# Layer 1's softplus begun inside layer 0's scan, its polynomial on POOL, B's rows before the slot fill, and filler products on PE

## The chip, the cores and the metric

The kernel runs on one core of a Trainium2 chip. The metric is device time in microseconds, median of several runs. Engines are named as in the profile: PE (TensorE, matrix products), DVE (VectorE), ACT (ScalarE), POOL (GpSimd), SP (issues most DMAs).

## What is computed

Four layers, each a residual attention-like part and a residual feed-forward part, each gated by a tanh. Tokens: 4 sequences of 256, so 1024 tokens, 256 features; everything is fp32. Layers 0 and 1 begin with a Mamba scan over `ctx_1024`:

```python
x = silu(conv(in_proj(ctx)) + conv_b)                 # u, 256 channels
dt_low, B, C = split(x_proj(x))                       # 8, 16 and 16 rows
delta = softplus(dt_proj(dt_low) + dt_b)
A = -exp(A_log)                                       # 256 x 16
state = state * exp(delta * A) + (delta * u) * B      # over 256 steps, for each of 16 states
y = (state * C).sum(states) + D * u
x_out = x + tanh(g) * y * silu(layernorm(x_in))
```

Behind them come a mixture of 16 experts (4 chosen, a router with sigmoid), a ternary feed-forward, an attention with 32 heads and an fp8 feed-forward, a second attention, and a mixture with 2 of 16 experts and a softmax router, of which only the chosen token rows are computed.

## The kernel before

The code is written engine by engine: each engine has one list of instructions, and they meet at counting semaphores alone (`wait_ge`, `then_inc`). Nothing reorders; what stands first on an engine runs first. Channels lie on the 128 partitions in two halves (`t` = 0, 1), tokens along the free dimension, so a half is 128x1024.

Both scans have 16 states. For each state and half ACT writes the decays exp(delta A) to PSUM (`decays`, L557), POOL multiplies delta u by the state's row of B (L588), which a DMA has spread over all partitions, DVE scans (L604) and weighs with C (L613), and PE adds up (L510). Layer 1's scan does not depend on x: it runs inside layer 0's mixture of experts (`mixture_*`), with POOL's L668 and L675 and DVE's L642 and L652.

Between them stands a chain. DVE forms y (L683, L687, two halves), PE turns it (L528, `mamba_tail_tensor`), DVE adds it to x and takes statistics (L691, L295, L299), POOL the inverse deviation (L312, L313), DVE normalises (L305, `ln_apply`), PE turns that (L322), ACT copies it to ZT (L330), PE makes the router's products (L1101) and the shared expert's (L733), and DVE chooses the experts (from L1142).

Softplus has three parts. ACT takes e = exp(-|d|) and e/3 - 1/2 (L436 to L441) and later ln(1 + e) (L445). DVE makes a mask e < 2^-7 and a polynomial (L453, L455, L456), puts the polynomial into the logarithm where the mask is set (L460), adds max(d, 0) (L461) and multiplies by u (L462); L466 is D u. For layer 1 ACT begins when the states of layer 0 are turned, and DVE's part stands between `ln_apply` and the router. POOL's first L668 waits for `du_done` and for a row of B. SP issues the rows of B and C for layer 1 behind `slot_dram <- slots`, a fill of 4 MB of DRAM that is used in the last mixture.

In the last mixture the router comes first again (L322 turns, the same L1101, softmax on DVE), the shared expert (L1279, L1289) runs on PE meanwhile, POOL scatters rows by indirect DMA (L1267), and 31 tiles of 128 slots go through turn (L1373), up (L1382), turn (L1391, L1392) and down products.

An fp32 product on PE is two instructions in the trace, a transpose one.

## Time and profile before

| what | value |
|---|---|
| median of 3 runs | 962.38 us (962.22 to 966.5) |
| profiled execution, its own time | 962.05 us |
| its span | 959.8 us |
| busy: PE, DVE, ACT, POOL | 85%, 70%, 46%, 45% of the span |
| chain that ended last: PE, DVE, issue, POOL, DMA, ACT | 50%, 29%, 9%, 5%, 3%, 3% |

The span is from the first to the last instruction of the profiled execution. The chain that ended last is followed back from the last instruction, at each step to what released it; its shares say where the time is set, while a busy share only says that an engine had work.

### The profile page before, as it was taken

The page shows a single profiled execution, that of the slowest core. Times are in us where ns is not written, and L with a number is a line of the kernel's source. Part 1 is how long each engine was busy: PE and PEld are TensorE (multiplying, and loading weights), DVE is VectorE, ACT ScalarE, POOL GpSimd, SP SyncE. Part 2 cuts the span into 40 slices and gives each one's busy share as a digit, 9 for nine tenths or more (in the row PEclk, how much of TensorE's full clock was granted, in tenths as well). Part 3 has the DMA queues.
Part 4 walks back from the last instruction along what each step waited for, and adds up shares of the span by engine and source line. Part 5 has one row for each costly group of instructions (what it writes and reads, how often), then busy time and mean ns, then how long its engine had stood idle before and what let it go on. Part 6 is the DMA issues. An engine that isn't in the chain of part 4 may idle for free.

```text
span 959.8 us, 12466 instructions
## 1 busy us (share of the span) xinstructions
PE 814.8 (85%) x4178; PEld 525.4 (55%) x4178; DVE 667.2 (70%) x1012; ACT 440.8 (46%) x826; POOL 433.2 (45%) x297
## 2 busy tenths in 40 slices
PE   7978989937999999982898979998937988979992
PEld 3323333335888877772776445554525865546661
DVE  5888999799999999997465467778537275312222
ACT  5752322350777767662555626665505422113331
POOL 3025666312599988883397012435301431513331
PEclk9977788867999999995899879999969986979997
DMA  6121122754122222211001113341161010151114
GB/s 224 50 86 68 66 66 76 295 203 131 44 88 89 88 88 87 88 44 43 35 1 34 52 39 93 98 134 36 56 238 33 1 67 1 71 194 49 46 44 158
DMA packets 28532, 81.71 MB, mean 85 GB/s; under 512 B 3360, under 2 KB 17200, under 8 KB 27088
## 3 DMA queue, kind: packets, MB, share of 16 engines
q1 hardware_dynamic: 26080, 73.25, 22.4%
q0 software_dynamic: 2256, 6.18, 1.8%
q10 hardware_dynamic: 144, 1.57, 0.4%
q8 instruction: 34, 0.56, 0.2%
q14 instruction: 18, 0.15, 0.1%
HBM read 65.64 MB, written 17.35 MB: 86 GB/s over the span
## 4 chain that ended last, share of the span: by engine, by line
PE 50%; DVE 29%; issue 9%; POOL 5%; DMA 3%; ACT 3%; DVEq 1%; SPq 0%; POOLq 0%; ACTq 0%
DVE M L652 6%; DVE M L642 6%; PE ps L510 6%; PE ps L1382 5%; PE ps L1752 4%; PE ps L1756 4%; PE ps L501 3%; PE ps L1794 3%; PE ps L384 3%; PE ps L934 3%; DVE F L873 2%; POOL ZT L1017 2%; PE ps L1401 2%; POOL slot_scratch L1267 2%; DVE stats L295 1%
## 5 line engine op out<-in xcount | busy, mean ns | idle before, releaser
L788 PE MATMUL ps<-W,ZT 128*128 128x256 f32 x512 | 122.1, 382 | 0.0
L588 POOL TENSOR_TENSOR M<-M 128x1024 f32<-128x1024 f32 x32 | 75.3, 2355 | 88.3 <-DVE M L462 47.4
L668 POOL TENSOR_TENSOR M<-N,M 128x1024 f32<-128x1024 f32 x32 | 81.9, 2561 | 55.4 <-DMA M<-dbl_scratch 39.1
L1823 ACT ACTIVATE N<-ps 128x512 f32<-128x512 f32 x128 | 69.5, 594 | 75.7 <-PE ps L1756 75.7
L788 PEld LDWEIGHTS ps<-W,ZT 128*128 128x128 f32 x512 | 93.5, 192 | 10.4
L675 POOL TENSOR_TENSOR W<-W,M 128x1024 f32<-128x1024 f32 x32 | 86.3, 2695 | 5.9 <-DVE M L652 5.9
L1844 DVE TENSOR_REDUCE W<-ps 128x4 f32<-128x1024 f32 x64 | 78.1, 1221 | 8.9 <-PE ps L1756 5.9
L1752 PE MATMUL ps<-M,W 32*128 32x256 f32 x512 | 74.0, 418 | 10.8 <-DVE W L1850 5.7
L510 PE MATMUL ps<-M,ident 128*128 128x512 f32 x128 | 75.7, 745 | 6.9 <-DVE M L613 6.9
L604 DVE TENSOR_TENSOR_SCAN M<-ps,M 128x1024 f32<-128x1024 f32 x32 | 73.3, 2291 | 9.0 <-ACT ps L557 8.4
L1756 PE MATMUL ps<-W,M 32*128 32x256 f32 x512 | 79.1, 402 | 0.0
L642 DVE TENSOR_TENSOR_SCAN M<-ps,M 128x512 f32<-128x512 f32 x64 | 77.8, 1216 | 0.8 <-issue 0.6
L557 ACT ACTIVATE ps<-M 128x1020 f32<-128x1020 f32 x32 | 35.7, 1115 | 81.6 <-DVE M L604 81.6
L810 PE MATMUL ps<-W,F 128*128 128x256 f32 x256 | 65.9, 380 | 1.0 <-ACT F L851 1.0
L652 DVE TENSOR_TENSOR M<-M 128x512 f32<-128x512 f32 x64 | 66.4, 1037 | 0.0
L1752 PEld LDWEIGHTS ps<-M,W 32*128 32x128 f32 x512 | 44.4, 191 | 38.2 <-DVE W L1850 19.2
L1007 POOL TENSOR_TENSOR M_rounded<-Z,M_rounded 128x512 fp32r<-128x512 f32 x28 | 40.4, 1446 | 51.4 <-ACT M_rounded L984 51.4
L934 PE MATMUL ps<-N_rounded,W_rounded 128*128 128x512 f32 x224 | 59.6, 413 | 3.2 <-DVE N_rounded L918 3.2
L1475 POOL DMA_INDIRECT ytok_scratch<-Z,M x31 | 29.8, 962 | 71.6 <-ACT Z L1437 71.6
L510 PEld LDWEIGHTS ps<-M,ident 128*128 128x128 f32 x128 | 29.0, 239 | 55.3 <-issue 43.6
L846 ACT ACTIVATE F<-F 128x128 f32<-128x128 f32 x128 | 55.5, 482 | 0.3
L1454 DVE COPY M<-ps 128x128 f32<-128x128 f32 x31 | 9.1, 292 | 66.4 <-PE ps L1392 66.4
(288 smaller groups left out, 1708.8 us busy)
## 6 DMA issues: line engine op xcount, KB each, us to landing
...
slot_scratch<-in_slots SPq DMA_DIRECT2D x1, 3999.0 KB, 18.6
...
```

The source lines that it names most:

```text
L510: last = nc.tensor.matmul(ps[:, 2 * t + half, :], ident[:], hC[:, t, half * HALF:(half + 1) * HALF], start=(n == 0), stop=True, skip_group ...
L588: nc.gpsimd.tensor_tensor(dBu[:, t, :], du[0][:, t, :], Bb[:, par, :], ALU.mult).then_inc(S("dBu_rdy"), 1)
L604: nc.vector.tensor_tensor_scan(hst[:, t, :], dAp, dBu[:, t, :], 0.0, ALU.mult, ALU.add).then_inc(S("h_rdy"), 1)
L642: nc.vector.tensor_tensor_scan(hst[:, t, at], dAp1[:, at], dBu[:, t, at], 0.0, ALU.mult, ALU.add).then_inc(S("h1_rdy"), 1)
L652: nc.vector.tensor_tensor(hC[:, t, at], hst[:, t, at], Cb[:, par, at], ALU.mult).then_inc(S("hC1_rdy"), 1)
L668: nc.gpsimd.tensor_tensor(dBu[:, t, :], du[1][:, t, :], Bb[:, par, :], ALU.mult).then_inc(S("dBu1_rdy"), 1)
L675: nc.gpsimd.tensor_tensor(u[1][:, t, :], u[1][:, t, :], hC[:, t, :], ALU.add).then_inc(S("y1_acc"), 1)
L788: last = nc.tensor.matmul(ps[:, UBANK[j % 2], e * DIM:(e + 1) * DIM], ZT[:, c, t * P:(t + 1) * P], gu[:, c, 2 * j + e, :], start=(c == 0), ...
L934: last = nc.tensor.matmul(ps[:, 4 + 2 * kind + q % 2, :], gu[:, c, u, kind * P:(kind + 1) * P], part[:, c, half * HALF:(half + 1) * HALF], ...
L1752: return nc.tensor.matmul(ps[:, b, q * SEQ:(q + 1) * SEQ], qst[32 * b:32 * b + 32, h, q * P:(q + 1) * P], kst[32 * b:32 * b + 32, h, :], s ...
L1756: return nc.tensor.matmul(ps[:, 4 + n % 3, k * SEQ:(k + 1) * SEQ], kst[32 * b:32 * b + 32, e, k * P:(k + 1) * P], qmax[32 * b:32 * b + 32, ...
L1844: nc.vector.tensor_reduce(spots[:, 2 * which:2 * which + 2], ps[:, 2 * which:2 * which + 2, :].rearrange("p b (q k) -> p b q k", q=2), AX. ...
```

## The change

On ACT the loop over layer 0's states is unrolled, and after states 10, 11 and 12 it takes one step of layer 1's softplus for both halves. The mask and the polynomial of layer 1 are on POOL, behind its last product of the first scan. The logarithm stands on ACT behind the two Silu of the tail; the first half's L460 and L461 stand on DVE before the tail and its L462 before the turned states, the rest where the softplus was. The rows of B for layer 1 are loaded once POOL is done with the rows of layer 0, with a semaphore of their own; the slot fill and `moe` are issued near the start, behind the first two rows of B; the rows of C wait for `du_done`. `stay_busy` puts products whose result nobody reads into eight waits of PE. On POOL three waits use the chain's semaphore.

```diff
+        log1 = two(W[:, w_free:w_free + 2 * TOK])
...
+        def stay_busy(bank, n):
+            for _ in range(n):
+                nc.tensor.matmul(ps[:, bank, :], ident[:], ctxT[:, 0:HALF], start=True, stop=True)
...
@@ mamba0_sync
+            sp.dma_start(moe[:, 0:MOE_COLS - 32], a["moe"]).then_inc(S("ld_w3"), 16)
+            sp.dma_start(slot_dram, a["slots"]).then_inc(S("ld_w3"), 16)
             with sp.Fori(1, NSTATE // 2) as i:
...
+        def mamba1_first_rows(sp):
             sp.wait_ge(S("dbl_out"), 32)
             sp.wait_ge(S("dBu_rdy"), 2 * NSTATE)
             for par in range(2):
-                load_rows(sp, 1, par, par)
+                sp.dma_start(Bb[:, par, :], row1(par)).then_inc(S("b1_in"), 16)
...
+        def softplus1_exponent(act, step):
+            for t in range(2):
+                if step == 0:
+                    nc.scalar.activation(Cb[:, t, :], delta[1][:, t, :], ACT.Abs).then_inc(S("sp_exp"), 1)
+                elif step == 1:
+                    act.wait_ge(S("sp_exp"), 6 + t + 1)
+                    nc.scalar.activation(log1[:, t, :], Cb[:, t, :], ACT.Exp, scale=-1.0).then_inc(S("sp_exp"), 1)
                 else:
+                    act.wait_ge(S("sp_exp"), 8 + t + 1)
+                    nc.scalar.activation(du[1][:, t, :], log1[:, t, :], ACT.Identity, scale=1.0 / 3.0,
+                                         bias=col("mhalf")[:, 0:1]).then_inc(S("sp_exp"), 1)
+        def softplus1_logarithm(act):
+            for t in range(2):
+                act.wait_ge(S("sp_poly"), t + 1)
+                nc.scalar.activation(log1[:, t, :], log1[:, t, :], ACT.Ln, bias=1.0).then_inc(S("sp_ln"), 1)
+        def softplus1_gpsimd(pool, link):
+            for t in range(2):
+                e, q = log1[:, t, :], du[1][:, t, :]
+                pool.wait_ge(S("sp_exp"), 10 + t + 1)
+                link(nc.gpsimd.tensor_scalar(Cb[:, t, :], e, 2.0 ** -7, None, ALU.is_lt))
+                link(nc.gpsimd.tensor_tensor(q, q, e, ALU.mult))
+                link(nc.gpsimd.tensor_scalar(q, q, 1.0, None, ALU.add))
+                nc.gpsimd.tensor_tensor(q, q, e, ALU.mult).then_inc(S("sp_poly"), 1)
+        def softplus1_delta(dve, link, t):
+            d, log = delta[1][:, t, :], log1[:, t, :]
+            dve.wait_ge(S("sp_ln"), 2 + t + 1)
+            link(nc.vector.copy_predicated(log, Cb[:, t, :].bitcast(mybir.dt.uint32), du[1][:, t, :]))
+            link(nc.vector.scalar_tensor_tensor(d, d, 0.0, log, ALU.max, ALU.add))
...
-            with act.Fori(1, NSTATE) as n:
-                decays(n, False)
+            for n in range(NSTATE):
+                decays(n, n == 0)
+                if 10 <= n < 13:
+                    softplus1_exponent(act, n - 10)
...
@@ sync
             sp.dma_start(dn, a["dn0"]).then_inc(S("ld_w0"), 16)
+            mamba1_first_rows(sp)
             sp.wait_ge(S("xm_done"), BATCH)
             sp.dma_start(tern, tern_dram).then_inc(S("tern_in"), 16)
-            sp.dma_start(moe[:, 0:MOE_COLS - 32], a["moe"]).then_inc(S("ld_w3"), 16)
-            sp.dma_start(slot_dram, a["slots"]).then_inc(S("ld_w3"), 16)
+            sp.wait_ge(S("du_done"), 4)
             mamba1_sync(sp)
@@ tensor
             mamba0_tensor(pe)
+            stay_busy(6, 5)
             mamba_tail_tensor(pe, 0)
+            stay_busy(3, 4)
             ln_tensor(pe, 1, 0)
+            stay_busy(3, 2)
             pe.wait_ge(S("ld_w0"), 80)
...
             pe.wait_ge(S("x_done"), NT)
+            stay_busy(2, 13)
             mamba_tail_tensor(pe, 1)
+            stay_busy(3, 4)
             pe.wait_ge(S("xm_done"), 2 * BATCH)
             ternary_tensor(pe)
+            stay_busy(7, 2)
...
             attn3_tensor(pe)
+            stay_busy(1, 3)
             ln_tensor(pe, 7, 5)
...
             pe.wait_ge(S("x_done"), 4 * NT)
             pe.wait_ge(S("expert_of"), 1)
+            stay_busy(0, 5)
             turn_rows(0)
```

Lines of the changed kernel are numbered anew. DVE behind the last weighing of the first scan (L613), before:

```order
L613 TENSOR_TENSOR M<-M,ps 128x1024 [waits y_acc,cb_rdy,h_rdy]
L683 SCALAR_TENSOR_TENSOR M<-M,cols,ps 128x1024 [waits y_acc,tanh_done]
L687 TENSOR_TENSOR M<-M 128x1024 [waits sz_done,dve_chain]
L683 SCALAR_TENSOR_TENSOR M<-M,cols,ps 128x1024
L687 TENSOR_TENSOR M<-M 128x1024 [waits sz_done,dve_chain]
L691 SCALAR_TENSOR_TENSOR X<-ps,tanh_g,X 128x512 [waits y_tr] x2
```

and in the changed kernel, where L667, L742, L746 and L752 are the old L613, L683, L687 and L691:

```order
L667 TENSOR_TENSOR M<-M,ps 128x1024 [waits y_acc,cb_rdy,h_rdy]
L515 COPY_PREDICATED W<-M,N 128x1024 [waits sp_ln]
L516 SCALAR_TENSOR_TENSOR N<-N,W 128x1024 [waits dve_chain]
L742 SCALAR_TENSOR_TENSOR M<-M,cols,ps 128x1024 [waits y_acc,tanh_done,dve_chain]
L746 TENSOR_TENSOR M<-M 128x1024 [waits sz_done,dve_chain]
L742 SCALAR_TENSOR_TENSOR M<-M,cols,ps 128x1024
L746 TENSOR_TENSOR M<-M 128x1024 [waits sz_done,dve_chain]
L519 TENSOR_TENSOR N<-N,W 128x1024
L752 SCALAR_TENSOR_TENSOR X<-ps,tanh_g,X 128x512 [waits y_tr,dve_chain]
```

L515 and L516, the old L460 and L461 of half 0, stand before the tail, and L519, the old L462, before the turned states.

DVE behind `ln_apply`, before, ten operations up to the second half's product:

```order
L453 TENSOR_SCALAR M<-M 128x1024 [waits sp_exp]
L455 TENSOR_TENSOR M<-M 128x1024 [waits sp_exp,dve_chain]
L456 SCALAR_TENSOR_TENSOR M<-M 128x1024 [waits dve_chain]
L453 TENSOR_SCALAR M<-M 128x1024 [waits sp_exp,dve_chain]
L455 TENSOR_TENSOR M<-M 128x1024 [waits sp_exp,dve_chain]
L456 SCALAR_TENSOR_TENSOR M<-M 128x1024 [waits dve_chain]
L460 COPY_PREDICATED M<-M 128x1024 [waits sp_ln,dve_chain]
L461 SCALAR_TENSOR_TENSOR N<-N,M 128x1024 [waits dve_chain]
L462 TENSOR_TENSOR N<-N,W 128x1024 [waits dve_chain]
L466 TENSOR_SCALAR W<-W,cols 128x1024 [waits dve_chain]
L460 COPY_PREDICATED M<-M 128x1024 [waits sp_ln]
```

and in the changed kernel (L522 is the old L466):

```order
L522 TENSOR_SCALAR W<-W,cols 128x1024
L515 COPY_PREDICATED W<-M,N 128x1024 [waits sp_ln]
L516 SCALAR_TENSOR_TENSOR N<-N,W 128x1024 [waits dve_chain]
L519 TENSOR_TENSOR N<-N,W 128x1024 [waits dve_chain]
L522 TENSOR_SCALAR W<-W,cols 128x1024 [waits dve_chain]
```

The polynomials and half 0 are gone from there.

POOL behind its last product of the first scan (L588), before:

```order
L312 TENSOR_SCALAR vpe<-mv 128x4 [waits ln_mv]
L313 TENSOR_TENSOR rstd<-vpe,cols 128x4 [waits pool_chain]
L312 TENSOR_SCALAR vpe<-mv 128x4 [waits ln_mv]
L313 TENSOR_TENSOR rstd<-vpe,cols 128x4 [waits pool_chain]
L668 TENSOR_TENSOR M<-N,M 128x1024 [waits bc0,du_done]
L668 TENSOR_TENSOR M<-N,M 128x1024
```

and in the changed kernel, where L313, L314 and L727 are the old L312, L313 and L668:

```order
L507 TENSOR_SCALAR M<-W 128x1024 [waits sp_exp]
L508 TENSOR_TENSOR N<-N,W 128x1024 [waits pool_chain]
L509 TENSOR_SCALAR N<-N 128x1024 [waits pool_chain]
L510 TENSOR_TENSOR N<-N,W 128x1024 [waits pool_chain]
L507 TENSOR_SCALAR M<-W 128x1024 [waits sp_exp]
L508 TENSOR_TENSOR N<-N,W 128x1024 [waits pool_chain]
L509 TENSOR_SCALAR N<-N 128x1024 [waits pool_chain]
L510 TENSOR_TENSOR N<-N,W 128x1024 [waits pool_chain]
L313 TENSOR_SCALAR vpe<-mv 128x4 [waits ln_mv]
L314 TENSOR_TENSOR rstd<-vpe,cols 128x4 [waits pool_chain]
L313 TENSOR_SCALAR vpe<-mv 128x4 [waits ln_mv]
L314 TENSOR_TENSOR rstd<-vpe,cols 128x4 [waits pool_chain]
L727 TENSOR_TENSOR M<-N,M 128x1024 [waits du_done,b1_in] x2
```

Eight operations of 128x1024 stand ahead of the inverse deviation, and the first L727 waits for half 0's `du_done` instead of half 1's.

## Rows read from the trace of the kernel before

**Rows 1.** Timeline of DVE: start, us, engine, line, idle before, releaser.

```profile
192.25 1.28 DVE L683 SCALAR_TENSOR_TENSOR M<-M,cols,ps 128x1024 f32<-128x1024 f32 x1 [2.20 <-PE ps L510]
...
198.45 1.60 DVE L691 SCALAR_TENSOR_TENSOR X<-ps,tanh_g,X 128x512 f32<-128x512 f32 x2 [1.21 <-PE ps L528]
...
207.90 0.69 DVE L453 TENSOR_SCALAR M<-M 128x1024 f32<-128x1024 f32 x1
...
214.39 1.36 DVE L460 COPY_PREDICATED M<-M 128x1024 f32<-128x1024 uint32 x1
...
217.04 1.23 DVE L462 TENSOR_TENSOR N<-N,W 128x1024 f32<-128x1024 f32 x1
...
223.80 0.29 DVE L1142 TENSOR_TENSOR Z<-Z,cols 128x128 f32<-128x128 f32 x1
...
226.59 2.31 DVE L1128 TENSOR_TENSOR M<-M,F 128x128 f32<-128x128 f32 x1
```

**Rows 2.** Timeline of PE in the same stretch.

```profile
214.26 6.98 PE L1101 MATMUL ps<-F,ZT 128*128 128x16 f32 x32 [5.20 <-ACT ZT L330]
```

**Rows 3.** Windows of PE: stretch, length, busy (instructions), granted clock, DMA share, GB/s.

```profile
436.00:438.00 2.00, 0.00 (x0) 0.50 0.00 0
464.00:468.00 4.00, 3.51 (x8) 0.50 0.00 0
```

**Rows 4.** Timeline of PE, from start, after the mixture, last router, experts.

```profile
12.34 14.01 PE L384 MATMUL ps<-M,W 128*128 128x512 f32 x32 [0.69 <-ACT M L411]
...
445.54 3.65 PE L528 MATMUL ps<-ident,M 128*128 128x128 f32 x16 [12.05 <-DVE M L687]
...
796.16 4.00 PE L322 MATMUL ps<-ident,M 128*128 128x128 f32 x16 [3.12 <-DVE M L305]
...
807.70 9.60 PE L1279 MATMUL ps<-ZT,W 128*128 128x512 f32 x16
...
847.21 0.66 PE L1373 MATMUL ps<-ident,M 128*128 128x128 f32 x2 [4.68 <-DMA M<-slot_scratch]
848.43 2.71 PE L1382 MATMUL ps<-W,M 128*128 x4 [0.56 <-ACT M L1423]
...
859.31 1.45 PE L1382 MATMUL ps<-W,M 128*128 x4
...
862.19 1.45 PE L1382 MATMUL ps<-W,M 128*128 x4
```

**Rows 5.** Timeline of ACT, in the first scan and behind it.

```profile
144.81 1.11 ACT L557 ACTIVATE ps<-M 128x1020 f32<-128x1020 f32 x1 [2.54 <-DVE M L604]
...
185.59 2.00 ACT L568 ACTIVATE M<-Z 128x1024 f32<-128x1024 f32 x2 [1.05 <-DVE M L604]
...
208.87 1.28 ACT L445 ACT_TABLE_LOAD   x1
```

**Rows 6.** Timeline of POOL, between the two scans.

```profile
201.99 0.23 POOL L312 TENSOR_SCALAR vpe<-mv 128x4 f32<-128x4 f32 x1 [21.22 <-DVE mv L299]
...
226.28 4.83 POOL L668 TENSOR_TENSOR M<-N,M 128x1024 f32<-128x1024 f32 x2 [19.71 <-DMA M<-dbl_scratch]
```

**Rows 7.** POOL by form: line, shapes, count, busy us, mean ns, idle before.

```profile
L1555 POOL TENSOR_SCALAR M<-M 128x768 f32<-128x768 f32 x6 | 16.7, 2775 | 0.5
...
L1262 POOL COPY M<-M 128x2048 f32<-128x2048 f32 x1 | 1.9, 1898 | 1.3 <-DVE M L305 1.3
```

**Rows 8.** Instructions of line 652: shortest, median and longest in ns, starts.

```profile
L652 DVE TENSOR_TENSOR M<-M x64: 666/930/2857, 247.1 to 431.3; 128x512 f32<-128x512 f32 x64
```

**Rows 9.** Timelines of POOL and DVE in the mixture, at 334 us.

```profile
334.20 2.35 POOL L668 TENSOR_TENSOR M<-N,M 128x1024 f32<-128x1024 f32 x1
...
334.29 2.82 DVE L652 TENSOR_TENSOR M<-M 128x512 f32<-128x512 f32 x1
```

**Rows 10.** DMA issues after 183 us: KB each, us from issue to landing.

```profile
slot_scratch<-in_slots SPq DMA_DIRECT2D x1, 3999.0 KB, 18.6
```

**Rows 11.** Windows of the queues in the first part: length, clock, DMA share, GB/s.

```profile
41.00:57.00 16.00, 0.99 0.00 1
```

More of the change, by code:

```diff
@@ L361, in mamba1_sync @@
             for par in range(2):
-                load_rows(sp, 1, par, par)
+                sp.dma_start(Bb[:, par, :], row1(par)).then_inc(S("b1_in"), 16)
+        def mamba1_sync(sp):
+            for par in range(2):
+                sp.dma_start(Cb[:, par, :], row1(par + NSTATE)).then_inc(S(f"bc{par}"), 16)
             with sp.Fori(1, NSTATE // 2) as i:
@@ L479, in softplus_vector @@
-            dve.wait_ge(S("delta_done"), 2 * (l + 1))
+                nc.vector.tensor_tensor(du[0][:, t, :], d, u[0][:, t, :], ALU.mult).then_inc(S("du_done"), 1)
+            dve.wait_ge(S("a_done"), 1)
+            nc.vector.tensor_scalar(Aneg, Aneg, -1.0, None, ALU.mult).then_inc(S("delta_done"), 1)
+            dve.wait_ge(S("u_done"), 3)
+            nc.vector.memset(dAp.rearrange("p (b l) -> p b l", b=BATCH)[:, :, 0:1], 0.0).then_inc(S("delta_done"), 1)
+            dve.wait_ge(S("delta_done"), 2)
@@ new lines, in softplus1_delta, with softplus1_drive, softplus1_skip @@
+        def softplus1_delta(dve, link, t):
[3 more added lines that the diff above has]
+            link(nc.vector.scalar_tensor_tensor(d, d, 0.0, log, ALU.max, ALU.add))
+        def softplus1_drive(dve, link, t):
+            link(nc.vector.tensor_tensor(du[1][:, t, :], delta[1][:, t, :], u[1][:, t, :], ALU.mult))
+        def softplus1_skip(dve, t):
+            nc.vector.tensor_scalar(u[1][:, t, :], u[1][:, t, :], col("D1")[:, t:t + 1], None,
+                                    ALU.mult).then_inc(S("du_done"), 1)
@@ L566, in mamba_tail_scalar @@
             act.wait_ge(S("z_done"), NT * (2 * l + 1))
+            if l == 0:
+                nc.scalar.activation(Aneg, col("alog1").rearrange("p (t n) -> p t n", t=2), ACT.Exp).then_inc(S("a_done"), 1)
             for t in range(2):
@@ L627, in mamba0_vector @@
             weigh_states(NSTATE - 1, 1, False)
+            softplus1_delta(dve, link, 0)
         def mamba1_piece(tile, j):
@@ L1022, in rms @@
                 pool.wait_ge(S("ssq_out"), half + 1)
-                nc.gpsimd.tensor_tensor(inv[:, at], sumsq[:, at], col("mhalf")[:, 0:4], ALU.pow).then_inc(S("rms_pow"), 1)
-                pool.wait_ge(S("rms_pow"), half + 1)
+                link(nc.gpsimd.tensor_tensor(inv[:, at], sumsq[:, at], col("mhalf")[:, 0:4], ALU.pow))
                 nc.gpsimd.tensor_tensor(tgi[:, at], inv[:, at], tanh_g[:, 5:6].to_broadcast([P, 4]),
@@ L2160, in _ @@
             ln_apply(dve, 1)
-            softplus_vector(dve, link, 1)
+            softplus1_skip(dve, 0)
+            softplus1_delta(dve, link, 1)
+            softplus1_drive(dve, link, 1)
+            softplus1_skip(dve, 1)
+            softplus1_rest(dve)
             dve.wait_ge(S("ld_w0"), 80)
```

81 lines of the change are left out of this document (38 added, 43 removed).

## The prediction

> **What bounds the kernel now.** The profiled execution took 962.05 us for a span of 959.8, so 2.25 us lie around the span; the median of the runs shown is 962.38. The page's chain of work (shares in the table above) lies half on PE and under a third on DVE, so no one engine bounds the whole and each edit must be priced where it stands. I read four places, each by the timeline of its engines.
>
> Place A, between the first scan and the mixture of experts. DVE waits 2.20 us for PE's accumulation, starts the tail at 192.25, waits 1.21 us for the turned states, normalises, and from 207.90 works through layer 1's softplus without a gap to the router, which it reaches at 223.80 [rows 1]. PE stands by: its router products take 6.98 us from 214.26 [rows 2], so the logits lie ready at 221.6. So DVE bounds this place, with 2.2 us to spare on PE.
> Places B to D are PE starting again after a wait. B at 445.54 after 12.05 us idle, C at 796.16 after 3.12, D at 847.21 after 4.68 [rows 4]. In B's wait the granted clock stands at 0.50 of full speed, which is 1.2 GHz, and at 464 to 468 it still does [rows 3]; PE holds up the pieces behind it there. In C the 16 transposes take 4.00 us, the last router's products fill the time to 807.70, another 7, and the first 16 shared products take 9.60, where 16 at the price of L384 (14.01 for 32) take 7.0. In D the first three tiles take 10.88 us (848.43 to 859.31), each later one 2.88 (862.19).
>
> **A, the work moved.** The two polynomials (L453, L455, L456, twice) hold DVE from 207.90 to 214.39: 6.49 us that go to POOL. L460 and L461 of the first half, 214.39 to 217.04, 2.65 us, move ahead of the tail. L462, 1.26 us with its gap, moves into the 1.21 us wait for the turned states, at no cost as long as that wait stands. Together 10.4 us leave the stretch between normalising and router [rows 1].
>
> On ACT six 128x1024 activations go between decays, two at a time, at states 10, 11 and 12. A pair of this shape takes 2.00 us (L568) and the gap between decays is 2.54 [rows 5]: hidden, up to 0.2 us if one pair overruns. Without that cover it would be 6.0 us, all on the scan.
>
> What comes back is the start of the tail. ACT: last scan over at 185.59, the 32 columns of Aneg (an estimated 0.2), table 1.28, two Silu 2.00, table 1.28, first Ln 1.00 [rows 5] gives 191.4. POOL is free at 201.99 - 21.22 = 180.8 [rows 6]; its polynomial is two tensor_scalar and two tensor_tensor a half. A tensor_tensor is 2.35 [rows 9]. A one-operation tensor_scalar of 1024 columns is not in the trace: from below the 128x2048 copy, 1.90, so 0.95; from above L1555, two operations on 768 columns, 2.78, so 3.7 scaled [rows 7]. I take 1.9, half way between by operations. The first half is ready at 187.7, 189.6 or 193.3, so Ln ends at 191.5, 191.5 or 194.4, and L460 with L461 ends at 194.2 or 197.1. The tail began at 192.25: 1.9 late, or 4.8.
> A second cost hides in the mixture. DVE's L652 takes 0.67 us at the shortest, 0.93 in the median and up to 2.86 [rows 8]. The one at 334.29 took 2.82: it started 0.09 us behind a POOL tensor_tensor of 2.35 and ended 0.56 us after it [rows 9]. I read this as exclusion: a DVE operation with two SBUF tensors waits for POOL's tensor_tensor to end, and the reverse. It also explains why L1128 took 2.31 us beside POOL's pair at 226.28, where L1142, the same shape, took 0.29: it and its successor L1129 stood behind one each, 2.02 us or 4.05 together [rows 1, 6]. In the changed kernel POOL's second half runs until 195 to 205, across L460, L461 and both L687. One collision costs about 2.3, two cost 4.6. With one to two the tail is late by 4.2 (cheap tensor_scalar) to 6; I take 5.0. POOL's two first products of the second scan then meet the rest of the softplus and the router: at most 4.7 us against 4.05 now, 0.4 lost.
> A = 10.4 - 5.0 - 0.4 = 5.0. Bounds: 8.4 without exclusion, and 1 if the tail is 7 late and PE at half clock throughout. PE check: transposes, two filler products, router products, read-out: behind the last normalised tile 0.3 + 1.7 + 3.5 + 0.3 = 5.8 us at full clock, 1.1 + 3.4 + 7.0 + 0.4 = 11.9 at half, where DVE needs 5.5 (five operations of the second half and the skip) plus a collision of 2.3 [rows 1, 2, 4]. At full clock nobody waits, at half clock PE is 4 us late, less 2 us of collisions that this time absorbs.
> The Trainium skill, GPSIMD Engine Reference, section 4.1 (engine selection), says that one-input operations run roughly at line rate and two-input ones about 2x slower than VectorE; by it tensor_scalar would be an estimated 1.1 us, and the sum 0.8 better. L1555 (2.78 for 768 columns) disagrees, for two operations.
>
> **B rows first, slot fill early.** B's rows of layer 1 now go out when POOL is done with the last product (180.8), behind the expert weights; they need to be there at about 215. The fill (18.6 us to landing) and moe go out at about 37, after the first two rows of B; the queues are empty from 41 to 57 (1 GB/s) [rows 10, 11], and the next row of B waits for a product of the scan. The landing that POOL waited for (19.71 us) ended at 226.28 [rows 6], and the scan it feeds comes only behind the router. Both edits: 0. If the fill were in the way, a row of B that lands late would stall the first scan by an estimated 4 us.
>
> **The filler products.** One is two instructions of 128x512: 32 such took 14.01 us [rows 4], so 0.88 us a product, 1.7 at half clock. 5, 4 and 2 of them are in A, priced above.
> B: 13 of them take 11.4 us. PE's wait is 12.05 [rows 4], of which DVE's last update of x, for which they wait, takes the first 0.5: 0 late at full clock. The clock already reads 0.50 at 436 though [rows 3], so it may fall before they start; one stretch of 3.3 us at half clock makes them 1.6 late. Gains: the 16 transposes 3.65 to 1.9 (0.6 reaches DVE, the next wait on DVE's own statistics), the ternary ones start ACT 1.2 sooner, L322 0.7, L934 half of the 3.5 us that it spends at 0.50, 1.7 [rows 3, 4]. Up to 4.2, less 0.7 for lateness and 0.8 where the clock does not hold: 2.7, bounds 0.5 and 4.2.
> C: three products, 2.6 us in a wait of 3.12. If all stays at full clock, the path to the end of the first 16 shared products (817.3), on which POOL's scatter hangs through the places, is shorter by 0.9 in L322, 3.5 in the router and 2.6 in the shared products, less 1.2 for what DVE sets: 5.8 [rows 4]. But the router's matmuls are 16 columns wide, and 32 of them took 6.98 us at the half-clock price [rows 2]. I expect it to fall in their midst: 2.3, bounds 0 and 5.8.
> D: five products start when DVE has made its last four updates of x, an estimated 1.7 us into the wait of 4.68, at 844.2, and end at 848.6, 1.35 later than the first tile's data (847.21 [rows 4]); that delay reaches the first up-product less 0.5 of faster transpose. In return the first three intervals, 10.88, fall to at most 8.64, and to an estimated 7.3 since the first ones lack the later parts: 3.6. Net 2.7, bounds 1.3 and 3.2.
> The `link` edits on POOL change only which semaphore counts: 0, since each waits for the same instruction.
>
> **Sum.** 5.0 + 2.7 + 2.3 + 2.7 = 12.7. Span 947.1, own time 949.3, against the median (0.33 above the profiled run) 949.7.
>
> The Trainium skill, TensorE: Matmul & The Clock Gate, Part 1, says that the default state is throttled and that activity releases it. By it filler helps only where it begins at full clock or lasts; if fillers (B's) start from the throttled state, the rule speaks against them, B would be an estimated 1.1 and the sum 11.1. The trace (0.50 at 436) leaves open which it is.
>
> **Rivals.**
> Port rival: exclusion does not bite (DVE's requests slip in first). Then A is 8.4: total 16.1, time 946.3. For it: the median L652 takes only 0.93 [rows 8]. Chance 0.2.
> Slow POOL: tensor_scalar 3.7 and collisions at each L687: the second half is ready at 206, the tail is 7 to 8 late, A is 2: time 952.7. For it: L1555. Chance 0.16.
> Clock rival: filler keeps nothing warm where it counts (narrow L1101, transposes), B, C, D give 2 together and A 3.5: 956.9. For it: in C neither 4.00 us of transposes nor 7 of router products brought full speed. Against it: the products of L384 ran at it. Chance 0.16. This holds also the case that the change does little.
> The other side: the 13 products of B all run at half clock and stand in front of the tail. They would take 22.4 us instead of 11.4 and put 11.0 us on the path, with A at 2 and C, D at 3: net 6 slower, 968. It decides from the point where more than half of the 13 run at half clock. Against it: 32 dense products of L384 took 0.44 us each, from PE's start on [rows 4]. Chance 0.04.
> Main case 0.44, its own range 946.5 to 952.5.
>
> **Numbers.** Range 943 to 957: from the best of the port rival with C and D full, to the clock rival. About 0.5% (4.8 us) is what a measurement of this kernel tells from no change: faster below 957.6. Main, port and slow POOL are all faster (0.80), of the clock rival a bit less than half: 0.86 faster; same 0.10; slower 0.04.
>
> **What would show it.** ACT: three pairs between decays, decay gaps unchanged. POOL: eight operations from 180.8, whose tensor_scalar gives the price that is missing. DVE: the tail's first operation at 196 to 198; L515 or L516 (the moved L460, L461) at 3.5 us where they meet POOL. Router start near 219 instead of 223.80. PE: granted clock 1.00 at B's transposes, L934 at 0.24 from the first, L1279's last of 16 2 to 6 us nearer to the router's start, and tiles every 2.9 us or less from the first. I am wrong if the tail starts at 192 to 194 (exclusion), if the fillers of B (L319 in the changed kernel) end well after the gated states are ready, or if the pieces of the mixture, which step by step are the same, change in length: four L652 of 2.4 to 2.9 us there show that the collisions depend on phase, which can shift 2 us either way.

## The result, and the profile after

| | before | changed |
|---|---|---|
| median of the runs | 962.45 us (962.22 to 966.5, 4 runs) | 950.56 us (948.56 to 955.26, 4 runs) |
| ratio, 95% interval | | 0.9874 (0.9829 to 0.9918) |
| profiled execution, span | 962.05, 959.8 | 950.15, 948.3 |

The forecast was 949.7. The total is right to 0.9 us; several of its terms are not, as the experiments show. The line numbers of the changed kernel are higher, by 54 in the first scan and by about 60 behind it. Of all executions behind this document one, of unroll_only, stands apart with 2652.57 us where its others took about 960; it is in no ratio.

DVE's timeline in place A (start, us, engine, line, idle before and releaser):

```profile
190.55 1.35 DVE L515 COPY_PREDICATED W<-M,N 128x1024 f32<-128x1024 uint32 x1 [3.96 <-ACT W L500]
191.94 1.23 DVE L516 SCALAR_TENSOR_TENSOR N<-N,W 128x1024 f32<-128x1024 f32 x1
193.20 1.28 DVE L742 SCALAR_TENSOR_TENSOR M<-M,cols,ps 128x1024 f32<-128x1024 f32 x1
194.51 1.93 DVE L746 TENSOR_TENSOR M<-M 128x1024 f32<-128x1024 f32 x1
...
197.67 1.22 DVE L746 TENSOR_TENSOR M<-M 128x1024 f32<-128x1024 f32 x1
...
211.60 3.21 DVE L516 SCALAR_TENSOR_TENSOR N<-N,W 128x1024 f32<-128x1024 f32 x1
...
218.28 0.06 DVE L529 MEMSET ps<- 128x4 f32 x1 [1.32 <-ACT Z L1173]
218.37 1.13 DVE L1202 TENSOR_TENSOR Z<-Z,cols 128x128 f32<-128x128 f32 x1
```

It answers to [rows 1]. The tail's first operation, L742, starts at 193.20 (192.25 before), although the last scan operation began 1.94 us sooner: relative to the scan it is 2.9 late. The two moved operations ahead of it wait for ACT's logarithm. L746 takes 1.93 where its twin takes 1.22. L516 takes 1.23 the first time and 3.21 the second. Then DVE stands 1.32 us for PE's logits, and the router starts at 218.37 instead of 223.80. POOL in the same stretch:

```profile
178.92 2.78 POOL L507 TENSOR_SCALAR M<-W 128x1024 f32<-128x1024 f32 x1
181.78 2.35 POOL L508 TENSOR_TENSOR N<-N,W 128x1024 f32<-128x1024 f32 x1
...
189.40 2.77 POOL L507 TENSOR_SCALAR M<-W 128x1024 f32<-128x1024 f32 x1
192.25 3.11 POOL L508 TENSOR_TENSOR N<-N,W 128x1024 f32<-128x1024 f32 x1
195.45 3.64 POOL L509 TENSOR_SCALAR N<-N 128x1024 f32<-128x1024 f32 x1
199.17 3.08 POOL L510 TENSOR_TENSOR N<-N,W 128x1024 f32<-128x1024 f32 x1
...
210.45 3.29 POOL L727 TENSOR_TENSOR M<-N,M 128x1024 f32<-128x1024 f32 x1 [2.22 <-DVE W L522]
```

L507 and L509 are the tensor_scalar on 128x1024 that the trace before did not have: 2.78 us where nothing is in its way. The L509 at 195.45 took 3.64, and it did so in all seven profiles with this polynomial: it began while DVE's first L746 still ran (to 196.44). The two halves of the polynomial end at 189.44 and 202.2. POOL's first product for the second scan, L727 at 210.45, is 3.29 us long where 2.35 is its price [rows 9]: it first waits for DVE's L515, and then L516 waits for it. ACT's three pairs of softplus steps lie between decays, as forecast:

```profile
145.69 1.99 ACT L488 ACTIVATE M<-N 128x1024 f32<-128x1024 f32 x2
...
152.78 1.99 ACT L491 ACTIVATE W<-M 128x1024 f32<-128x1024 f32 x2
...
159.88 2.17 ACT L494 ACTIVATE N<-W,cols 128x1024 f32<-128x1024 f32 x2
```

PE at B, C and D (the groups that begin with L319 are fillers; a row x24 or x10 counts instructions), and the windows of the same places (stretch, length, busy with instructions, granted clock, DMA share, GB/s):

```profile
425.17 11.43 PE L319 MATMUL ps<-ctxT,ident 128*128 128x512 f32 x26 [0.58 <-DVE X L942]
436.55 1.97 PE L579 MATMUL ps<-ident,M 128*128 128x128 f32 x16
...
454.08 7.41 PE L995 MATMUL ps<-N_rounded,W_rounded 128*128 128x512 f32 x24 [1.90 <-DVE N_rounded L979]
...
784.66 2.74 PE L319 MATMUL ps<-ctxT,ident 128*128 128x512 f32 x6
...
792.09 5.79 PE L1161 MATMUL ps<-F,ZT 128*128 128x16 f32 x32 [0.74 <-ACT ZT L336]
...
834.78 4.56 PE L319 MATMUL ps<-ctxT,ident 128*128 128x512 f32 x10 [1.75 <-DVE X L1388]
839.17 0.38 PE L1433 MATMUL ps<-ident,M 128*128 128x128 f32 x2
...
847.44 1.45 PE L1442 MATMUL ps<-W,M 128*128 x4
```

```profile
425.00:445.00 20.00, 17.87 (x70) 1.00 0.10 34
...
455.00:459.00 4.00, 4.00 (x13) 0.57 0.01 4
793.00:803.00 10.00, 10.00 (x33) 0.52 0.00 0
835.00:855.00 20.00, 18.53 (x71) 1.00 0.68 218
```

It answers to [rows 3, 4]. B: the 26 filler instructions run at full clock and take 11.43 us, L579 takes 1.97 (3.65 for the same turn before), but L995 is 7.41 long, with the clock at 0.50 from 455.5 to 458.9, after the last fillers. C: the clock falls in the midst of the router's L1161. D: the fillers start 1.75 us after PE ran dry and end at 839.3; then the fourth up-product group stands at 847.44 and the clock is 1.00 throughout.

### The profile page after: what moved, and what is told of

The parts are those of the page before. It is cut to its first block, busy times and chain, and to the rows that moved or that the text cites. A ratio compares the mean times of both kernels' runs of the same rounds, so it can differ in the third digit from the quotient of the medians.

```text
span 948.3 us, 12525 instructions
## 1 busy us (share of the span) xinstructions
PE 835.6 (88%) x4254; PEld 528.5 (56%) x4254; DVE 661.2 (70%) x1006; ACT 438.3 (46%) x825; POOL 455.9 (48%) x305
## 4 chain that ended last, share of the span: by engine, by line
PE 48%; DVE 30%; issue 8%; POOL 4%; DMA 4%; ACT 4%; SPq 1%; DVEq 1%; POOLq 0%; ACTq 0%
DVE M L707 6%; DVE M L697 6%; PE ps L1442 5%; PE ps L1812 4%; PE ps L561 4%; PE ps L995 4%; PE ps L1816 4%; PE ps L1854 3%; PE ps L1339 3%; PE ps L552 2%; DVE F L934 2%; PE ps L319 2%; PE ps L1461 2%; PE ps L1007 2%; PE ps L1728 1%
## 5 line engine op out<-in xcount | busy, mean ns | idle before, releaser
L849 PE MATMUL ps<-W,ZT 128*128 128x256 f32 x512 | 120.9, 379 | 0.0
L1883 ACT ACTIVATE N<-ps 128x512 f32<-128x512 f32 x128 | 69.5, 595 | 78.0 <-PE ps L1816 78.0
L727 POOL TENSOR_TENSOR M<-N,M 128x1024 f32<-128x1024 f32 x32 | 83.0, 2594 | 41.4 <-DVE M L697 18.1
L1812 PE MATMUL ps<-M,W 32*128 32x256 f32 x512 | 76.8, 433 | 11.2 <-DVE W L1910 6.0
L1904 DVE TENSOR_REDUCE W<-ps 128x4 f32<-128x1024 f32 x64 | 78.1, 1221 | 11.5 <-PE ps L1816 8.2
L1816 PE MATMUL ps<-W,M 32*128 32x256 f32 x512 | 82.0, 414 | 0.0
L658 DVE TENSOR_TENSOR_SCAN M<-ps,M 128x1024 f32<-128x1024 f32 x32 | 73.3, 2290 | 7.7 <-ACT ps L608 3.2
L1812 PEld LDWEIGHTS ps<-M,W 32*128 32x128 f32 x512 | 46.4, 201 | 39.0 <-DVE W L1910 19.9
L707 DVE TENSOR_TENSOR M<-M 128x512 f32<-128x512 f32 x64 | 67.5, 1055 | 0.0
L1068 POOL TENSOR_TENSOR M_rounded<-Z,M_rounded 128x512 fp32r<-128x512 f32 x28 | 40.4, 1444 | 49.1 <-ACT M_rounded L1045 49.1
L995 PE MATMUL ps<-N_rounded,W_rounded 128*128 128x512 f32 x224 | 58.0, 405 | 3.7 <-DVE N_rounded L979 3.7
L1816 PEld LDWEIGHTS ps<-W,M 32*128 32x128 f32 x512 | 55.4, 192 | 2.7 <-issue 1.2
```

The lines of the kernel that those rows point to most:

```text
L658: nc.vector.tensor_tensor_scan(hst[:, t, :], dAp, dBu[:, t, :], 0.0, ALU.mult, ALU.add).then_inc(S("h_rdy"), 1)
L707: nc.vector.tensor_tensor(hC[:, t, at], hst[:, t, at], Cb[:, par, at], ALU.mult).then_inc(S("hC1_rdy"), 1)
L727: nc.gpsimd.tensor_tensor(dBu[:, t, :], du[1][:, t, :], Bb[:, par, :], ALU.mult).then_inc(S("dBu1_rdy"), 1)
L849: last = nc.tensor.matmul(ps[:, UBANK[j % 2], e * DIM:(e + 1) * DIM], ZT[:, c, t * P:(t + 1) * P], gu[:, c, 2 * j + e, :], start=(c == 0), ...
L995: last = nc.tensor.matmul(ps[:, 4 + 2 * kind + q % 2, :], gu[:, c, u, kind * P:(kind + 1) * P], part[:, c, half * HALF:(half + 1) * HALF], ...
L1812: return nc.tensor.matmul(ps[:, b, q * SEQ:(q + 1) * SEQ], qst[32 * b:32 * b + 32, h, q * P:(q + 1) * P], kst[32 * b:32 * b + 32, h, :], s ...
```

## The experiments

Twelve runs, in four groups that each ran on one chip beside the kernel before. The times of one kernel spread more than the first table suggests (the kernel before ran from 955.7 to 971 us in these groups), so I read each also by stages. The table is worked out from starts of instructions in the timelines:

- scan: from the start to the last scan operation of layer 0;
- A: from there to the first scan operation of layer 1;
- Mix: to the last product of the mixture;
- B: to the first product of the attention's scores (L1812, before L1752), so with the feed-forward in it;
- C0: to the turn of C. This is the attention, where nothing was edited;
- CD: to the first turn of D;
- D6: to the sixth up-product; then the rest.

Each row is one execution, not the median. The profiled one of no_filler took 6.4 us more than its kernel's median, that of filler_only 5.6, of pool_late 6.6 and of d_only 3.0, that of after_again 3.3 less.

| kernel | scan | A | Mix | B | C0 | CD | D6 | rest | span |
|---|---|---|---|---|---|---|---|---|---|
| before | 183.3 | 59.5 | 190.8 | 122.7 | 239.9 | 51.1 | 17.9 | 94.7 | 959.8 |
| filler_only | 183.7 | 60.2 | 193.3 | 121.7 | 242.0 | 55.8 | 14.0 | 94.9 | 965.6 |
| d_only | 184.4 | 58.3 | 191.9 | 120.1 | 243.8 | 50.8 | 14.1 | 94.6 | 958.2 |
| unroll_only | 182.9 | 57.9 | 189.4 | 121.4 | 242.3 | 51.2 | 17.7 | 94.8 | 957.6 |
| no_filler | 181.9 | 53.4 | 192.5 | 122.1 | 244.6 | 51.2 | 17.8 | 95.2 | 958.8 |
| changed | 181.3 | 52.9 | 190.4 | 120.3 | 243.0 | 51.2 | 14.0 | 95.1 | 948.3 |
| after_again | 180.4 | 51.9 | 188.3 | 119.4 | 241.3 | 55.5 | 14.0 | 95.0 | 945.8 |
| pool_late | 179.2 | 53.1 | 197.1 | 120.3 | 245.9 | 56.8 | 14.0 | 95.5 | 961.8 |
| d_three | 179.3 | 52.7 | 192.5 | 117.4 | 243.9 | 54.2 | 14.0 | 95.1 | 949.1 |
| no_d | 181.1 | 52.1 | 190.7 | 118.8 | 243.1 | 49.9 | 18.0 | 95.1 | 948.7 |
| d_ahead | 180.5 | 52.0 | 188.7 | 121.2 | 243.5 | 48.2 | 14.1 | 95.3 | 943.4 |
| short_poly | 182.9 | 49.8 | 187.6 | 121.7 | 242.2 | 55.8 | 14.0 | 94.7 | 948.7 |
| best1 | 179.8 | 50.0 | 190.1 | 120.9 | 241.1 | 48.3 | 14.1 | 94.9 | 939.3 |
| best2 | 181.8 | 50.7 | 188.1 | 117.8 | 242.9 | 50.0 | 14.1 | 94.8 | 940.1 |

### no_filler: the moved work without the fillers

```diff
-            stay_busy(6, 5)
...
-            stay_busy(1, 3)
```

> The changed kernel without any filler product; everything else of the change stays. Theory 1 (what the fillers gave is local and is what the two profiles show at B, C and D: 1.5, 1.3 and 2.4 us, and at A the logits, which DVE waited 1.3 us for although 6 filler products had kept PE at work, come 1 to 2 us later): 950.6 + 5.2 + 1.5 = 957.3 us, between 955.5 and 959. Rival (moved work and fillers only shift where PE's half-speed stretches fall, and the gains at B to D are luck of one execution): within 1.5 us of 950.6. Also read: the last scan operation of layer 0 starts at 181.3 us, as in the changed kernel, if the unrolled loop on ACT shortens the scan, and anywhere between 181 and 184 if PE's clock sets it.

Measured: 954.24 us, before 962.88 in the same group, ratio 0.9914 (0.9884 to 0.9944), so 8.3 us (5.4 to 11.2) come without any filler; the edit takes out all eight calls. It lies between the two theories, and fits neither. The logits do come later: DVE waits for PE 2.27 us instead of 1.32. Stage A is 53.4 us, against 52.9 in the changed kernel: A does not hang on its fillers.

### filler_only: B, C and D without the moved work

```diff
+            stay_busy(2, 13)
             mamba_tail_tensor(pe, 1)
+            stay_busy(3, 4)
...
+            stay_busy(7, 2)
...
             attn3_tensor(pe)
+            stay_busy(1, 3)
...
             pe.wait_ge(S("expert_of"), 1)
+            stay_busy(0, 5)
```

> The kernel before with only the fillers of B, C and D (13 + 4 + 2, 3 and 5). Theory 1 (local gains): 962.4 - 5.2 = 957.2 us, between 956 and 959.5; the attention part between 540 and 570 us is then the same length as in the kernel before. Rival (fillers bring a longer half-clock stretch 100 us later, as the profile after shows with 3 us in the attention part): 960 us. Rival 2 (gains at B to D are luck): 962. The last scan operation of layer 0 starts at 183.3 us if the unrolled loop on ACT was what shortened the scan in the changed kernel.

Measured: 962.22 us, before 962.88, ratio 0.9995 (0.9965 to 1.0024), so 0.5 us, at most 3.4. The theory of local gains, on which 7.7 of my 12.7 us rested, is out for the sum; rival 2 (962) has the number. The table says where: D6 is 3.9 shorter, and CD is 4.7 longer. Beside the moved work the fillers were worth more: the ratios of no_filler (0.9914) and of the changed kernel (0.9874 and 0.9902) differ by 1 to 4 us, inside their intervals.

### pool_late: is it exclusion?

```diff
-                pool.wait_ge(S("du_done"), 3 + t)
+                pool.wait_ge(S("du_done"), 4)
```

> The changed kernel with POOL's first product of the second scan held back until both halves of du are done, about 4 us later. Theory (exclusion: DVE's L516 of 3.21 us stood behind POOL's product of 3.29): L516 takes 1.23 us, DVE is 2.0 us sooner at the router, of which PE's late logits leave at most 0.7; the product now stands in the router's first operations. Time 950.6, between 949.5 and 951.5. Rival (L516 is slow for another reason, such as its operands): it stays at 3.2 us. Rival 2 (the scan waits for that product): up to 3 us slower.

Timelines of DVE and POOL:

```profile
209.51 1.23 DVE L516 SCALAR_TENSOR_TENSOR N<-N,W 128x1024 f32<-128x1024 f32 x1
...
216.20 0.06 DVE L529 MEMSET ps<- 128x4 f32 x1 [3.33 <-ACT Z L1173]
216.30 1.42 DVE L1202 TENSOR_TENSOR Z<-Z,cols 128x128 f32<-128x128 f32 x1
...
212.93 4.65 POOL L727 TENSOR_TENSOR M<-N,M 128x1024 f32<-128x1024 f32 x2 [6.79 <-DVE W L522]
```

L516 takes 1.23 us: exclusion holds. The router's L1202 is 1.42 instead, and PE's logits come 3.33 us later than DVE could use them, so A does not gain. The kernel took 957.01 us (ratio 0.9949, 0.9916 to 0.9982), which none of the three theories gave. In the profiled execution, 6.6 us above that median, the mixture alone, whose instructions are the same, is 197.1 us long against 188.3 in after_again. DVE's groups of L707 in the mixture (busy us, mean ns; after_again, then pool_late):

```profile
L707 DVE TENSOR_TENSOR M<-M 128x512 f32<-128x512 f32 x64 | 64.2, 1003 | 0.0
```

```profile
L707 DVE TENSOR_TENSOR M<-M 128x512 f32<-128x512 f32 x64 | 73.3, 1145 | 0.0
```

64 operations of 0.67 us at the shortest take 64.2 or 73.3 us. In six of the profiles (after_again, d_ahead, before, no_d, no_filler, pool_late) the mixture's length follows this number: 64.2, 65.2, 66.4, 67.3, 68.5, 73.3 us busy, with lengths of 188.3, 188.7, 190.8, 190.7, 192.5, 197.1. The other eight fit as well: in all fourteen the mixture is these 64 operations and 122.7 to 124.8 us more. How DVE's products fall against POOL's is worth up to 9 us. No edit was aimed at it; whether holding POOL's first product back brought the 73.3 about, or chance did, is not shown.

### d_three: fewer fillers at D

```diff
-            stay_busy(0, 5)
+            stay_busy(0, 3)
```

> The changed kernel with three fillers instead of five ahead of the expert tiles. Theory (the five end 1.46 us after the first tile's rows are ready, and two fewer end 1.8 us sooner, with the clock still up): first transposed rows 1.4 us earlier, 949.2 us. Rival (with three the clock falls within the first three tiles): those take 10.9 us instead of 7.3 and the kernel is 952.4 to 953.

Measured: 952.78 us, ratio 0.9914 (0.9877 to 0.9951). That is the rival's number without its mechanism: the clock holds with three (D6 14.0), yet the first turn comes later than in the changed kernel, CD 54.2 against 51.2. The last update of x (L1388) started 3.1 us after PE's last product had ended, with a releaser that the profile calls remote, which is to say that it names none on this core; the fillers are queued behind the wait for it.

### after_again: the changed kernel once more

> The changed kernel once more, unaltered, as the yardstick of this group. Theory (half-speed stretches of PE fall by chance, and they, not the edits, set the first scan and the attention part): its last scan operation of layer 0 starts anywhere from 179 to 184 us (181.32 in the first profile, 179.2 and 179.3 in two kernels whose first 180 us are the same code), and its times spread over 950 to 963 us with a median near 955. Rival (the edits fix the schedule): 181.3 again and a median within 1 us of 950.6.

Measured: 950.94 us (947.64 to 953.05), before 960.94, ratio 0.9902 (0.9871 to 0.9932). The median is the rival's, within 1 us of 950.6; the scan's end is not (180.4). Against the first profile the scan's end moved by 1 us, the mixture by 2, and D by 4. DVE and PE at D:

```profile
827.60 1.66 DVE L1388 SCALAR_TENSOR_TENSOR X<-ps,tanh_g,X 128x256 f32<-128x256 f32 x4 [7.32 <-remote]
...
829.31 7.60 PE L319 MATMUL ps<-ctxT,ident 128*128 128x512 f32 x10 [4.63 <-DVE X L1388]
836.75 0.38 PE L1433 MATMUL ps<-ident,M 128*128 128x128 f32 x2
```

The update comes 7.32 us after DVE's last work instead of 4.44, PE has by then been idle for 4.63 us, and the ten filler instructions take 7.60 us instead of 4.56, partly at half clock (0.50 from 829). The first turn waits for them all: 836.75.

### d_ahead: the same fillers, ahead of the wait

```diff
+            stay_busy(0, 5)
             pe.wait_ge(S("x_done"), 4 * NT)
             pe.wait_ge(S("expert_of"), 1)
-            stay_busy(0, 5)
```

> The changed kernel with the five fillers of D ahead of the wait for the last update of x instead of behind it. Theory (they now run in the wait, and an update that comes 3 us late, as in four of six profiles, no longer pushes them into the path): the first turn comes 4.4 us behind the end of the last scatter issue, where the changed kernel has 5.9 and d_three 8.9; the six tiles still take 14.0 us. 1.5 to 4.6 us faster than the changed kernel in the same group, 3 in the mean. Rival (PE is idle for 4 to 8 us between fillers and tiles, the clock falls, and the tiles take 17.9 us): no faster, up to 2 us slower.

Measured: 945.6 us in after_again's group, ratio 0.9838 (0.9806 to 0.9869), 5.3 us faster than the changed kernel, a little more than the 1.5 to 4.6 expected.

```profile
832.02 1.66 DVE L1388 SCALAR_TENSOR_TENSOR X<-ps,tanh_g,X 128x256 f32<-128x256 f32 x4 [7.21 <-remote]
...
829.06 4.46 PE L319 MATMUL ps<-ctxT,ident 128*128 128x512 f32 x10
833.99 0.41 PE L1433 MATMUL ps<-ident,M 128*128 128x128 f32 x2 [0.48 <-DMA M<-slot_scratch]
```

The update is as late (7.21), but the fillers run in its shadow at full clock and the turn now waits 0.48 us for the rows to land, nothing else. D6 stays at 14.1.

### no_d and d_only: D's fillers alone, taken out and put in

```diff
# no_d, against the changed kernel
-            stay_busy(0, 5)
# d_only, against the kernel before
+            stay_busy(0, 5)
             pe.wait_ge(S("x_done"), 4 * NT)
```

> The changed kernel without the five fillers of D. Theory (behind the wait for the last update of x they cost more than they bring: from the turn of C to the sixth up-product 69.5 us in the repeated profile, of which 55.5 up to the first turn; without them 48.6 and 17.9): 66.5 us for that stretch and 948 us, 3 us faster than the changed kernel (950.9). Rival (the reading of the first profile, where D's fillers gave 2.4 us): 953.3 us.

> The kernel before with five fillers of D alone, ahead of the wait for the last update of x. Theory: the first turn comes when the rows have landed, as in the kernel before, and the six tiles take 14.0 us instead of 17.9: 3.8 us faster than before in the same group. Rival (other half-speed stretches take the place): under 1 us.

Measured: no_d 950.42 us, ratio 0.9883 (0.9838 to 0.9927); d_only 957.41, ratio 0.9964 (0.9936 to 0.9992), 3.5 us faster (0.8 to 6.2). For no_d neither the theory (948) nor the rival (953.3) came. CD and D6 together are 67.9 in no_d, where the changed kernel has 65.2 and 69.5. As they stand in the changed kernel D's fillers are worth 2.7 us in one profile and cost 1.6 in the other; in the medians nothing can be told. Ahead of the wait they are worth 3.5 us by d_only.

### short_poly: half the work on POOL

```diff
-                    nc.scalar.activation(du[1][:, t, :], log1[:, t, :], ACT.Identity, scale=1.0 / 3.0, ...
+                    nc.scalar.activation(du[1][:, t, :], log1[:, t, :], ACT.Square, scale=3.0 ** -0.5, ...
+                else:
+                    nc.scalar.activation(du[1][:, t, :], du[1][:, t, :], ACT.Identity, bias=sp_const[:, 1:2])
...
-                link(nc.gpsimd.tensor_tensor(q, q, e, ALU.mult))
-                link(nc.gpsimd.tensor_scalar(q, q, 1.0, None, ALU.add))
...
+            softplus1_logarithm(act, 0)
             mamba_tail_scalar(act, 0)
-            softplus1_logarithm(act)
+            softplus1_logarithm(act, 1)
```

> The changed kernel with a shorter polynomial: ACT squares (e/1.732 - 0.433) and adds 0.8125, at states 10 to 13, so that POOL has one tensor_scalar and one tensor_tensor a half instead of two and two; the first half's logarithm stands ahead of the two Silu on ACT. Theory (the tail waits for the POOL and ACT chain: 11.88 us from the last scan to the tail against 8.99 before): POOL is done at 189.2 instead of 202.2, the distance is 9.0 us again, and L746 takes 1.22 us instead of 1.93: 2.9 to 3.6 us faster than the changed kernel in the same group. Rival (PE's accumulation or a collision of L516 with POOL holds the tail at 11 us or more): under 1 us.

DVE (the moved operations are L518 and L519 here) and POOL:

```profile
187.99 1.22 DVE L670 TENSOR_TENSOR M<-M,ps 128x1024 f32<-128x1024 f32 x1 [1.68 <-PE ps L564]
189.12 2.24 DVE L518 COPY_PREDICATED W<-M,N 128x1024 f32<-128x1024 uint32 x1
191.40 1.22 DVE L519 SCALAR_TENSOR_TENSOR N<-N,W 128x1024 f32<-128x1024 f32 x1
...
193.98 1.22 DVE L749 TENSOR_TENSOR M<-M 128x1024 f32<-128x1024 f32 x1
...
187.78 2.36 POOL L513 TENSOR_TENSOR N<-N,W 128x1024 f32<-128x1024 f32 x1
```

L749, the former L746, takes 1.22 us, and the tail starts 9.8 us after the last scan operation with PE's accumulation 1.68 us late (9.0 was expected); A is 49.8 against 51.9. L518, a copy_predicated, is 2.24 long beside POOL's tensor_tensor that ends at 190.14, 1.22 before it ends itself: it is excluded too. The median, 951.14 (0.9903, 0.9872 to 0.9934), shows none of the 2.1 us; the scan before it was 2.5 us longer in this profile. The next section has the same edit on top of d_ahead, and there it is worth 4.8 us (945.6 to 940.79). So its worth in the median stays open; in stage A it shows each time (49.8, 50.0 and 50.7 against 51.9 to 53.4).

### best1 and best2: both edits, and POOL's last two operations exchanged

```diff
# best1: short_poly with d_ahead. best2, against best1:
-  mask(0), times_e(0), mask(1), times_e(1)
+  mask(0), times_e(0), times_e(1), mask(1)
```

> Both edits together (short polynomial, fillers of D ahead of the wait). If both theories hold: 5 to 6.5 us faster than the changed kernel in the same group, about 949 us. If only the first: 3.

> The combined version with POOL's last two operations of the polynomial exchanged (product of the second half first, its mask last), so that the first half's L519 on DVE stands beside a tensor_scalar and not beside a tensor_tensor. Theory (exclusion is between POOL's tensor_tensor and DVE operations with two SBUF operands): L519 takes 1.23 us instead of 3.23, tail 9.0 us or less behind the last scan operation, 0.5 to 2 us faster than best1 (940.8). Rival (POOL's tensor_scalar excludes DVE as well): L519 stays above 2.5 us, no change.

Measured: best1 940.79 us, ratio 0.9791 (0.976 to 0.9821), 10.2 us faster than the changed kernel in the same group; best2 942.26 in the next group, ratio 0.9806 (0.9765 to 0.9847), no different by these intervals. The 10.2 are more than the 5 to 6.5 expected, and more than the two edits gave alone (none and 5.3). In best1 one collision was left, on DVE and POOL:

```profile
186.34 3.23 DVE L519 SCALAR_TENSOR_TENSOR N<-N,W 128x1024 f32<-128x1024 f32 x1
...
185.39 3.10 POOL L513 TENSOR_TENSOR N<-N,W 128x1024 f32<-128x1024 f32 x1
```

In best2 that operation took 1.22 us, but PE's accumulation was 2.6 us late and POOL was done by then, so it proves nothing of the exchange. That a running tensor_scalar on POOL does not hold up DVE is shown by the first two listings: L515 at 190.55 lies inside L507 (189.40, 2.77) and takes 1.35, and the second L746, at 197.67, lies inside L509 (195.45, 3.64) and takes 1.22. The other way round it does not hold: L509 waited for the first L746, whose end at 196.44 and the 2.78 of a free tensor_scalar give 199.2, where it ended at 199.09.

### unroll_only: a term that I had not seen

DVE's waits in the first scan (us in total, times, longest), before and changed. L604 and L658 are the scan operations, L613 and L667 the weighing:

```profile
DVE M L604 <- ACT ps L557: 8.4, 23, 2.6
DVE M L613 <- PE ps L501: 3.6, 5, 1.5
```

```profile
DVE M L658 <- ACT ps L608: 3.2, 11, 1.2
DVE M L667 <- PE ps L552: 3.1, 3, 1.5
DVE M L658 <- POOL M L642: 2.4, 1, 2.4
```

The long wait of 2.4 to 2.6 is the same one, once put down to POOL. Without it DVE waits 5.8 us for ACT before and 3.2 after, 22 times against 11. The view lists no wait shorter than about 0.15 us, and that matters here: by starts and lengths in the timelines the idle times before the scan operations mostly alternate between 0.25 and 0.17 us with the loop, and between 0.16 and 0.13 us written out, where the shorter ones drop out of the view. All of them together, short ones too and without the long first one, are 6.5 us before and 5.3 in the changed kernel.

```diff
-            decays(0, True)
-            with act.Fori(1, NSTATE) as n:
-                decays(n, False)
+            for n in range(NSTATE):
+                decays(n, n == 0)
```

> The kernel before with ACT's loop over the states of the first scan written out, nothing else. Theory (the loop costs ACT time at each decay, for which DVE's scan waits: 21 to 23 waits and 8.0 to 8.4 us on ACT and POOL in the three profiles that have the loop, 11 to 14 waits and 5.6 to 5.9 in those of four that have none and no long stall): 5.6 us here too, the last scan operation starts at 181 to 182 us instead of 183.3 to 184.5, and the kernel is 2 to 2.5 us faster than before in the same group. Rival (PE's half-speed stretches alone make the difference): the waits on ACT and POOL stay at 8 us, no change in time.

```profile
DVE M L612 <- PE ps L501: 3.8, 5, 1.5
DVE M L603 <- ACT ps L557: 2.9, 9, 1.2
DVE M L603 <- POOL M L587: 2.4, 1, 2.4
```

The waits on ACT and POOL are 5.3 us in the view; all idle time before the scan operations, as above, is 5.2 us against 6.4 to 6.5 in the three profiles with the loop. So the loop costs 1.3 us. The kernel took 959.79, ratio 0.9966 (0.9936 to 0.9995), 3.3 us (0.5 to 6.2) faster than before, which holds the 1.3 as well as the 2 to 2.5 expected. The scan's end at 182.9 missed the 181 to 182: PE's waits (3.8) were as long as with the loop.

## Why the forecast was right, and where not

**Sum.** The two profiles differ by 11.5 us: scan 1.9, A 6.6, mixture 0.4, B 2.4, D6 3.8, and against that C0 -3.1, CD -0.2, the rest -0.4. I forecast 12.7. It came out because a term that I had at 0 (the scan) and one that I had too low (A) made up for fillers that bring far less than 7.7. That the total fits to 0.9 us is luck in part: the errors have opposite signs.

**A, 5.0 forecast, 6.6 in the pair.** Over all profiles it is 6.4: 59.0 in the mean of the four kernels without the moved work (57.9 to 60.2), 52.6 in the seven with it and the long polynomial (51.9 to 53.4). The 10.4 us left as said. Back came 2.9 by the tail, 0.7 by L746, 2.0 by L516 and 1.3 by PE's logits; given back were 3.2 where L1128 and L1129 no longer stand behind POOL (4.05, now 0.84 at L1202): 10.4 - 6.9 + 3.2 = 6.7. So the tail's lateness with its collision was 3.6, not 5.0. The price that I took for POOL's tensor_scalar, 1.9, was 2.78, so the first logarithm waited for POOL. That the tail was nonetheless less late than 5.0 lies in the collisions: one, and L746 only partly hit (0.7), instead of one to two of 2.3.

The step that failed is the one on POOL's two first products of the second scan, put at 0.4 lost: they met less, 2.0 at L516 and 0.84 at L1202, 2.8 against 4.05, so 1.2 gained. That hangs on another term, the rows of B, which I had at 0: before, their landing ended POOL's wait for these products (19.71 us, [rows 6]), and now it is DVE's L522 (2.22). How much of it is the rows' and how much the earlier first half is open; no run takes that edit out. And PE was late by 1.32: the case "at half clock" of my check came true in part, with the clock at 0.50 from 210 to 213 and from 217.

The Trainium skill, GPSIMD Engine Reference, section 4.1, has one-input operations roughly at line rate, which made an estimated 1.1 us. The trace has 2.78 for the tensor_scalar against 2.35 for the two-input tensor_tensor, so the measurement decides against it.

**Exclusion.** Shown by L516 (3.21 and 1.23 with one wait changed), L746, and L518 and L519 of short_poly and best1. The port rival is out. It is mutual: L727 at 210.45 took 3.29. An operation of DVE that reads PSUM is not held: L742, at 193.20 inside L508, took 1.28 as before.

**First scan, 0 forecast.** Missed: the diff unrolls ACT's loop, which I listed and did not price. It is worth 1.3 us, shown by unroll_only. The scan ends at 183.8 in the mean of the three profiles with the loop (183.3 to 184.4) and at 181.0 in the eleven without (179.2 to 182.9). The rest of that is DVE waiting less for PE's accumulation, 1.4 to 4.7 us without the loop against 4.3 to 4.6 with it; why it varies so is open. The three inserted pairs cost nothing, as said.

**B, 2.7 forecast.** Stage B is 121.6 us in the mean of the four profiles without its fillers (120.1 to 122.7) and 120.0 in the ten with them (117.4 to 121.7): 1.6, with a spread above it. L995 gained nothing (7.44 before, 7.41): the clock fell again behind the last fillers. **C, 2.3.** CD is 51.1 in the mean of the four without C's fillers, and 48.2, 48.3, 49.9 and 50.0 where C's fillers stand and D's don't get in the way: 2.0.

**D, 2.7.** The gain was as said: 3.8 off the first tiles in every profile. The term "that delay reaches the first up-product" was mis-sized: 1.35 forecast; by CD (55.0 in the mean of the five kernels with five fillers behind the wait, 51.2 to 56.8, against 49.1 in the four with C's fillers and none there) it is 5.9. B, C and D together make 1.6 + 2.0 + 3.8 - 5.9 = 1.5, near the 2 of the clock rival, but not by its mechanism: D's tiles did run at full clock. It hangs on DVE's update being on time, and the update was 3 us late in all twelve profiles of the experiments and in neither of the first two (DVE idle for 6.6 to 7.4 us ahead of it, against 4.44). What holds it up is open: no_filler and unroll_only, which have no fillers, show it as well.

**What was not edited.** I had warned of 2 us either way in the mixture; it is 9. C0 is 239.9 in the profile of before and 241 to 246 in the thirteen others, so the 3 us that the changed kernel seemed to lose in the attention look like the luck of that one execution of before: PE stood at half clock for 10 us between the first L1752 and the last weighing of the attention then, and for 15 to 21 in the thirteen, d_only and unroll_only among them, which edit nothing near. The Trainium skill, TensorE: Matmul & The Clock Gate, Part 1, has the throttled state as the default from which activity releases; here B's fillers began at 1.00 and held it (11.43 us for 26), those of after_again's D began after 4.63 us of idle PE and ran in part at 0.50. Both agree with it.
